# Adapter product between the turns and the scores, the next slot's turn behind the values, q's parts in two pairs of buffers

## The reference

```python
W = weights[condition]; h = einsum('bct,bcd->bdt', x, W)           # style, one 32x32 matrix a batch
qkv = clip(h @ w_qkv.T, -8, 8); q, k = layer_norm(q), layer_norm(k) # over 512 features
scores = q k^T / 4 + alibi bias, causal; probs = softmax(scores)    # 32 heads of 16, 32x32 each
x = x + (probs v) @ w_out.T
y = einsum('bsi,boi->bso', x, weight[adapter_ids])                  # one 512x512 matrix a batch
shared = relu(y @ up_w) ** 2 @ down_w
routed = (y @ fc1 @ expert @ fc2) * sum(top2(y @ gate_w))
x = x + layer_norm(shared + routed)
```

## Time and profile before

| | us |
|---|---|
| median of 3 runs (1119.55 to 1126.66) | 1122.88 |
| the profiled execution | 1121.46 |
| its span, first to last instruction | 1119.7 |
| attention loop, iterations 6 to 30 | 469.47 |

### The profile page before, as it was taken

The page is one execution under the profiler, slowest core; times in us unless marked ns, Lnnn a source line. Parts: engine busy times, 40 slices in busy tenths (PEclk is TensorE's granted clock), DMA queues, the critical chain, the costliest instruction groups (busy, mean ns, idle before and its releaser), DMA issues.

```text
span 1119.7 us, 28302 instructions
## 1 busy us (share of the span) xinstructions
PE 1080.5 (97%) x11396; PEld 874.3 (78%) x11396; DVE 672.4 (60%) x1040; ACT 600.7 (54%) x985; POOL 714.0 (64%) x612
## 2 busy tenths in 40 slices
PE   6999999999999999999998999999999999999994
PEld 4778878788887888877777778787878888787883
DVE  5677667576766677666656245565656565554432
ACT  4567677577776777786866415334161625233220
POOL 4666888788887888888665463555465563533332
PEclk9999999999999999999999999999999999999997
DMA  7125555456555557656467952243315123030101
GB/s 278 41 80 193 196 178 196 167 188 192 186 184 187 187 191 206 193 180 196 151 237 266 346 156 85 85 111 109 97 47 144 49 92 97 29 85 29 47 29 38
DMA packets 95297, 160.84 MB, mean 144 GB/s; under 512 B 46401, under 2 KB 47169, under 8 KB 89793
## 3 DMA queue, kind: packets, MB, share of 16 engines
q1 hardware_dynamic: 79456, 118.16, 32.7%
q0 software_dynamic: 12224, 34.10, 9.6%
q10 hardware_dynamic: 3488, 6.78, 1.7%
HBM read 93.97 MB, written 42.47 MB: 122 GB/s over the span
## 4 chain that ended last, share of the span: by engine, by line
PE 95%; issue 1%; DMA 1%; SPq 1%; DVE 1%; POOL 0%; ACT 0%; DVEq 0%; POOLq 0%
PE banks L675 16%; PE banks L860 16%; PE pair L884 16%; PE bank L675 8%; PE bank L724 7%; PE bank L790 7%; PE banks L877 4%; PE bank L877 4%; PE bank L665 3%; PE banks L790 3%; PE pair L692 3%; PE pair L752 3%; PE banks L830 1%; PE banks L735 1%; PE banks L771 1%
## 5 line engine op out<-in xcount | busy, mean ns | idle before, releaser
L1756 POOL TENSOR_TENSOR w_lo<-w2t,w_hi 128x2048 fp32r<-128x2048 f32 x38 | 174.7, 4598 | 39.4 <-ACT w_hi L1057 36.5
L1826 POOL TENSOR_TENSOR u_lo<-act,u_hi 128x512 fp32r<-128x512 f32 x64 | 82.7, 1292 | 102.6 <-ACT u_hi L1257 102.5
L675 PE MATMUL banks<-wqkv_hi,h_hi 128*128 128x512 f32 x256 | 104.4, 408 | 0.2
L860 PE MATMUL banks<-yT_hi,up_hi 128*128 128x512 f32 x256 | 100.8, 394 | 1.2 <-DMA yT_hi<-y_part_high 1.2
L675 PE MATMUL banks<-wqkv_lo,h_hi 128*128 128x512 f32 x256 | 100.6, 393 | 0.0
L675 PE MATMUL banks<-wqkv_hi,h_lo 128*128 128x512 f32 x256 | 100.5, 392 | 0.0
L860 PE MATMUL banks<-yT_hi,up_lo 128*128 128x512 f32 x256 | 99.8, 390 | 0.0
L860 PE MATMUL banks<-yT_lo,up_hi 128*128 128x512 f32 x256 | 99.6, 389 | 0.0
L884 PE MATMUL pair<-down_hi,u_hi 128*128 128x512 f32 x256 | 99.6, 389 | 0.0
L884 PE MATMUL pair<-down_lo,u_hi 128*128 128x512 f32 x256 | 99.6, 389 | 0.0
L884 PE MATMUL pair<-down_hi,u_lo 128*128 128x512 f32 x256 | 99.6, 389 | 0.0
(11 more groups left out here) (217 smaller groups left out, 3048.3 us busy)
## 6 DMA issues: line engine op xcount, KB each, us to landing
w2t<-in_w SPq DMA_DIRECT2D x38, 1024.0 KB
vx<-v_hl SPq DMA_DIRECT2D x128, 68.0 KB
x1g<-x_rows SPq DMA_DIRECT2D x32, 256.0 KB, 2.9
kx<-k_hl SPq DMA_DIRECT2D x124, 64.0 KB
x_rows<-x1t SPq DMA_DIRECT2D x31, 256.0 KB
ffn_high<-w_high SPq DMA_DIRECT2D x20, 256.0 KB, 3.5
ffn_low<-w_low SPq DMA_DIRECT2D x20, 256.0 KB, 3.6
stage<-in_wqkv SPq DMA_DIRECT2D x3, 1024.0 KB, 9.4
```

The costliest lines, as they stand in the source:

```text
L675: m = e.matmul(into, a[:, c, :], b[:, n, c, :], start=(c == 0 and k == 0), stop=(c == KC - 1 and k == 2))
L860: i = e.matmul((B2, B3)[n % 2], a[:, w, cols], b[m % 2][:, c, :], start=(c == 0 and k == 0), stop=(c == KC - 1 and k == 2))
L1756: e.tensor_tensor(w2_lo[:, :, :], w2t[:, :, :], w2_hi[:, :, :].bitcast(F32), ALU.subtract).then_inc(d_wlo, 1)
L1826: e.tensor_tensor(u_lo[n % FC][:, :], act[n % 2][:, :], u_hi[n % FC][:, :].bitcast(F32), ALU.subtract) \
```

## The change

- On TensorE `adapt_slot(i-6)` moves ahead of `scores(i-2)`; the turn of a slot moves from ahead of `turn_values` to the end of the iteration before, behind `values` (`turn_slot(i-5)` in iteration i, for i from 5 to 29).
- `q_hi`, `q_lo` exist twice; `high_q(t)` and `low_q(t)` wait for `scores(t-2)`.
- `high_chunk` copies to B6 behind `add_x(n)`, and `style` waits for its reader `low_chunk`; the waits on `r_low` at the turns go.
- ScalarE: `slot_in` is the iteration's first; `scale_q` stands ahead of `high_h`; `high_v` behind `high_k`; the planes behind `slot_out`, and their last pair behind `high_o(T-5)`.
- VectorE: `low_slot` stands ahead of `take_k`; `bias_max` behind `low_k`; `low_planes` behind `bias_max`.
- GpSimd: `gather_slot` waits for `style(i+1)` on TensorE and not for `scores(i-2)`; for i = 1 to 3 `style` stands ahead of the gathers.
- SP: `load_planes` behind `load_w2`, `keep_planes` behind `spread_k`.

The diff, with one line of context:

```diff
--- before.py
+++ after.py
@@ -201,8 +201,7 @@
...
     vf = [asb(f"vf{i}", [P, DM]) for i in range(2)]
-    q_hi = asb("q_hi", [P, KC, P], BF16)
-    q_lo = asb("q_lo", [P, KC, P], BF16)
+    q_hi, q_lo = [asb("q_hi0", [P, KC, P], BF16)], [asb("q_lo0", [P, KC, P], BF16)]
 
@@ -304,6 +303,11 @@
...
     u_tiles(range(5, FC))
+    second_q = ExitStack()
+    qsb = tiles_in(second_q)
+    q_hi.append(qsb("q_hi1", [P, KC, P], BF16))
+    q_lo.append(qsb("q_lo1", [P, KC, P], BF16))
+    second_q.close()
     gates = sb("gates", [2 * EXPERTS, TOK])
@@ -575,14 +579,12 @@
...
                     keep_chunk(i - 5)
-                if i >= T - 8:
-                    keep_planes(i - T + 8)
-                if i >= T - 9:
-                    load_planes(i - T + 9)
                 if 0 <= i - 4 < CHUNKS:
...
                     load_w2(i - 5)
+                if i >= T - 9:
+                    load_planes(i - T + 9)
                 if i == 1:
@@ -590,17 +592,19 @@
...
                     spread_k(i - 1)
+                if i >= T - 8:
+                    keep_planes(i - T + 8)
 
...
             load_back(0, 0, 0, 3)
-            keep_planes(EARLY_GROUPS * KC - 1)
             upto(e, "tq", T - 2)
...
             spread_k(T - 2)
+            keep_planes(EARLY_GROUPS * KC - 1)
             upto(e, "tq", T - 1)
@@ -661,6 +665,8 @@
...
                 upto(e, "hlo", t - 1)
+                if t > 5:
+                    e.wait_ge(r_low, min(t - 5, CHUNKS))
                 for c in range(KC):
@@ -697,10 +703,8 @@
...
                 upto(e, "olo", t - 1)
-                if t:
-                    e.wait_ge(r_low, min(t, CHUNKS))
-                if t + 4 > LAG:
-                    e.wait_ge(d_tl, min(t + 4 - LAG, LAST))
+                if t + 4 >= LAG:
+                    e.wait_ge(d_tl, min(t + 5 - LAG, LAST))
                 for b in range(BPT):
@@ -743,8 +747,9 @@
...
                 upto(e, "on", t - 2)
+                hi, lo = q_hi[t % 2], q_lo[t % 2]
                 for c in range(KC):
-                    for k, (a, n) in enumerate(((q_hi, 0), (q_lo, 0), (q_hi, 1))):
+                    for k, (a, n) in enumerate(((hi, 0), (lo, 0), (hi, 1))):
                         for j in range(BPT):
@@ -763,7 +768,6 @@
...
                     upto(e, "olo", s + LAG - 5)
-                    e.wait_ge(r_low, min(s + LAG - 4, CHUNKS))
                 for c in range(KC):
@@ -945,8 +949,6 @@
...
                 project_v(i)
-                if i >= LAG:
-                    turn_slot(i - LAG, banks47)
                 if i >= 4:
@@ -956,16 +958,18 @@
...
                     style(i + 1)
+                if i >= LAG:
+                    adapt_slot(i - LAG, B5)
                 if i >= 2:
                     scores(i - 2)
-                if i >= LAG:
-                    adapt_slot(i - LAG, B5)
                 if i >= 4:
...
                     values(i - 3)
+                if LAG - 1 <= i < T - 2:
+                    turn_slot(i - LAG + 1, banks47)
 
@@ -1045,7 +1049,6 @@
...
                 if slot_halved(s):
-                    upto(e, "ot", s + LAG - 4)
                     e.activation(whole(xgT_hi[:, :]), half(banks47, 0), ACT.Copy).then_inc(d_tc, 1)
@@ -1069,10 +1072,8 @@
...
                 e.activation(w_high[:, :], w_raw[:, :], ACT.Copy).then_inc(r_high, 1)
-                upto(e, "olo", n)
-                if n + 5 > LAG:
-                    e.wait_ge(d_tl, n + 5 - LAG)
-                e.activation(B4, w_raw[:, :], ACT.Copy).then_inc(r_bank, 1)
+                upto(e, "x1", n)
+                e.activation(B6, w_raw[:, :], ACT.Copy).then_inc(r_bank, 1)
 
@@ -1182,8 +1183,8 @@
...
                 upto(e, "qT", t)
-                upto(e, "s", t - 1)
-                e.activation(q_hi[:, :, :].rearrange("p c (g t) -> p c g t", g=ROW_TILES), q_at(t), ACT.Copy) \
+                upto(e, "s", t - 2)
+                e.activation(q_hi[t % 2][:, :, :].rearrange("p c (g t) -> p c g t", g=ROW_TILES), q_at(t), ACT.Copy) \
                     .then_inc(A["qhi"], 1)
@@ -1209,6 +1210,8 @@
...
             for i in range(T - 1):
+                if i >= LAG:
+                    slot_in(i - LAG, banks47)
                 if i < SHORT:
@@ -1222,27 +1225,30 @@
...
                     high_chunk(i - 5)
-                if i >= T - 8:
-                    join_planes(i - T + 8)
-                    high_planes(i - T + 8)
                 if i >= LAG:
...
                     normalize(i - 1)
-                if i >= LAG:
-                    slot_in(i - LAG, banks47)
                 if i >= 4:
                     high_o(i - 4)
-                high_v(i)
-                if i >= SHORT:
+                if i < LAG:
+                    high_v(i)
+                if SHORT <= i < LAG:
                     high_h(i + 1)
...
                     scale_q(i - 1)
+                if i >= LAG:
+                    high_h(i + 1)
+                if i >= 1:
                     scale_k(i - 1)
...
                 if i >= LAG:
+                    high_v(i)
                     slot_out(i - LAG, B5)
+                if i >= T - 8:
+                    join_planes(i - T + 8)
+                    high_planes(i - T + 8)
                 if i >= 2:
@@ -1261,8 +1267,6 @@
...
             high_probs(T - 4)
-            join_planes(EARLY_GROUPS * KC - 1)
-            high_planes(EARLY_GROUPS * KC - 1)
             high_w2(LAST)
@@ -1274,6 +1278,8 @@
...
             high_o(T - 5)
+            join_planes(EARLY_GROUPS * KC - 1)
+            high_planes(EARLY_GROUPS * KC - 1)
             scale_k(T - 2)
@@ -1370,7 +1376,7 @@
...
                 e.wait_ge(r_bank, n + 1)
-                e.tensor_tensor(w_low[:, :], B4, w_high[:, :].bitcast(F32), ALU.subtract).then_inc(r_low, 1)
+                e.tensor_tensor(w_low[:, :], B6, w_high[:, :].bitcast(F32), ALU.subtract).then_inc(r_low, 1)
 
@@ -1378,7 +1384,6 @@
...
                 if slot_halved(s):
-                    upto(e, "ohi", s + LAG - 4)
                     e.tensor_tensor(whole(lo), half(banks47, 0), whole(hi), ALU.subtract).then_inc(d_tl, 1)
@@ -1398,8 +1403,8 @@
...
                     upto(e, "khi", t)
-                upto(e, "s", t - 1)
-                parts = [q[:, :, :].rearrange("p c (g t) -> p c g t", g=ROW_TILES) for q in (q_hi, q_lo)]
+                upto(e, "s", t - 2)
+                parts = [q[t % 2][:, :, :].rearrange("p c (g t) -> p c g t", g=ROW_TILES) for q in (q_hi, q_lo)]
                 e.tensor_tensor(parts[1], q_at(t), parts[0], ALU.subtract).then_inc(A["qlo"], 1)
@@ -1574,25 +1579,27 @@
...
                     low_chunk(i - 5)
-                if i >= T - 8:
-                    low_planes(i - T + 8)
+                if i >= LAG:
+                    low_slot(i - LAG, banks47)
                 take_k(i)
...
                     low_weights(3)
-                if i >= LAG:
-                    low_slot(i - LAG, banks47)
                 if i >= 4:
...
                     low_h(i + 1)
-                if i >= 2:
+                if 2 <= i < LAG:
                     bias_max(i - 2)
...
                     low_k(i - 1, k_hl)
+                if i >= LAG:
+                    bias_max(i - 2)
+                if i >= T - 8:
+                    low_planes(i - T + 8)
                 if i >= 4:
@@ -1792,11 +1799,13 @@
...
                     e.wait_ge(s_tables, 2)
+                if 0 < i < SHORT:
+                    style(i + 2)
                 if i + 3 < T:
...
                     gather_style(i + 3)
-                if i < SHORT:
-                    style(i + 2)
+                if i == 0:
+                    style(2)
                 if i == 0:
@@ -1808,7 +1817,10 @@
...
                 if i >= LAG - 1:
-                    upto(e, "s", i - 2)
+                    if i + 1 < T:
+                        upto(e, "h", i + 1)
+                    else:
+                        upto(e, "s", i - 2)
                     gather_slot(i - LAG + 1)
...
                     subtract_max(i - 2)
```

## The result

The kernel after takes 1173.43 us (median of 4 runs, 1173.03 to 1174.18); the kernel before, beside it, 1122.97 (4 runs, 1119.55 to 1126.66). The ratio is 1.045, with a 95% interval of 1.042 to 1.048. The forecast was 1137, 1118 to 1153: slower was right, and the time lies 36 us over it.

A forecast was written before the change was run, and what follows sets the result against it. It took TensorE, busy 459.46 of 469.47 us in the attention loop, as the bound. Loop +14.5, gather +1.5, slow products −1.6 and tail +0.8 gave +15.2 on 1121.5: 1137, range 1118 to 1153.

The forecast's parts named there:

- A loop through the swapped product, the row maximum and `w_lo`: Attention loop: period 19.6 us through iteration 24, then 18.6, against TensorE's own 18.45; likeliest case, chance 0.74.
- `w_lo` end to product: Loop term: from the end of `w2_lo` on GpSimd to TensorE's first adapter product, 0.21 us.
- bias and row maximum: Loop term on VectorE: from the bias's start to the row maximum's end, 2.53 us.
- row maximum to the next `w_lo` end: Loop term: subtraction, Exp, transpose, copies and `w2_hi` through the end of `w2_lo`, 13.04 us.
- late 11.99: Stretch from row maximum to `w2_lo` end after iteration 24, when no chunk is copied: 11.99 us.
- rival (d): TensorE's clock falls at each recurring 1.1 us wait, slowing the product: +38 us, 1175; chance 0.05.
- scores 1.08: Loop term: scores 0.93 us start to start, plus 0.15 until VectorE starts the bias.
- the gather's start at 3.92 behind `w_lo`'s end: GpSimd's slot gather starts 3.92 us after `w2_lo` ends; used to work out when it lands.
- Product 2.91 and not 2.72: Loop term: the adapter's twelve products on TensorE, forecast at 2.72 us, bounds 2.72 to 2.97.
- Rival (c): Slot's gather lands behind the 1 MB load and decides the period: at 5.5 us landing, 1152; chance 0.09.
- it also fails if VectorE's low_q, low_k hold up the bias: Failure sign on VectorE: these low parts delay the bias, lengthening the loop by their lateness; no size given.
- The stops without a semaphore: Unexplained TensorE waits, about 7 of 10 us; up to 7 could return, most hidden by the loop.

The follow-up runs named there:

- low_last: Kernel after, with the adapter's four products with `w2_lo` last, only those waiting for it, and the `w2t` load waiting for the whole product: 1170.7 us.
- swap_back: Kernel after, with `scores(i-2)` ahead of `adapt_slot(i-6)` again and all else still changed: 1161.6 us.
- before_swap: Kernel before, with only `adapt_slot(i-6)` moved ahead of `scores(i-2)`: 1153.1 us.
- turn_back: Kernel after, with the slot's turn and its readers back at the head of the next iteration's turns, ahead of `turn_values`: 1159.4 us.
- swap_back_bias_first: Kernel after, with scores ahead of the product and bias and row maximum ahead of `low_q`, `low_k` on VectorE; turn still behind `values`: 1144.8 us.
- gather_early: Kernel after, with GpSimd issuing the slot's gather ahead of `reciprocals` and `low_probs`: 1163.4 us.
- gather_after_scores: Kernel after, with the slot's gather waiting for `scores(i-2)` again: 1165.1 us.
- after_gather_early_bias_first: Kernel after, with the gather ahead of `reciprocals` and bias and row maximum first on VectorE; both TensorE moves stay: 1156.6 us.
- before_qk_first: Kernel before, with only VectorE's order changed from iteration 6 on: `low_q` and `low_k` ahead of bias and row maximum: 1162.7 us.

## Why the prediction was right and wrong

**Right.** A loop through the swapped product, the row maximum and `w_lo` sets the period. Its terms, forecast and measured: `w_lo` end to product 0.21, 0.22; bias and row maximum 2.53, 2.55; row maximum to the next `w_lo` end 13.04, 12.96, late 11.99 and 12.31 (the subtraction took 2.28 and not the 1.91 of the earlier trace rows). TensorE waits before its product in nearly every iteration. The clock stays at 1.00, so rival (d) is out in this kernel; that its 1175 lies near is chance. In kernels where TensorE waits longer its mechanism does appear (low_last, swap_back). Alone the loop has 19.7 us (before_swap) where 19.6 was forecast.

**Wrong, the term that carries the miss:** "scores 1.08". The scores with their bias took 2.36, because GpSimd issues the slot's gather inside them. The forecast had the gather's start at 3.92 behind `w_lo`'s end, and the scores from 2.93 to the bias at 4.01 behind it (0.21 + 2.72 + 1.08), and never laid the two beside each other. It costed the gather's new wait by its landing alone. In the kernel before nothing had to keep them apart: the scores stood ahead of the product, and in the earlier trace rows the gather starts with no wait but its own 0.17. With the product ahead, the old wait for the scores would have done it: in before_swap the gather starts 4.7 behind the product's start and the scores have no stop. Product 2.91 and not 2.72 adds 0.19. So the period is 21.0 and not 19.6, and later 20.35 and not 18.6 (there the subtraction's 2.28 adds 0.3 too): 18 × 1.4 + 6 × 1.75 = 36 us, the whole distance from 1137 to 1173. (The sum starts from the profiled execution, 1.4 under the median, and leaves these 1.4 out: by its own terms it is 1138.) The size of the stops is measured, but they couldn't have been worked out from rows: the same issue costs 0.2 plus 0.3 us in turn_back.

**Rival (c) was not a rival, but a second limit.** It was priced with a landing of 4.0 from the earlier trace rows and a bound of 5.1. Where TensorE waits for it, the landing is over the bound: 5.9 in the row of swap_back_bias_first above. In the kernel after, landings of 3.5 to 5.1 us are traced and one of 6.3. They hardly show, because the loop at 21.0 leaves time for them: the turn comes 9.0 behind the product's start and not 7.7. The Trainium skill (DMA: Bandwidth & Descriptors, Anatomy of one DMA) fits about 2.0 us plus bytes over 436 GB/s for a GpSimd DMA, an estimate of 2.6 for the gather's 256 KB; the measured 5.9 includes whatever the load beside it adds.

**Named but not followed:** "it also fails if VectorE's low_q, low_k hold up the bias". In the kernel after they end at 218.92, 1.79 before the bias starts, so the forecast's step held. Without the stops the scores would end some 1.3 earlier, and the margin would be 0.5; in gather_early it is used up in many iterations. With the product behind the scores the bias is held by 4 us. It is the third limit.

**How they combine.** With the other two removed, VectorE's order costs 26 us (1142.1 against 1116.3), the turn 28 (1144.8 against 1116.3) and the swap 35 (1156.6 against 1121.9, where the turn stays behind values but its gather is early). The last two each hold three iterations with the clock at 0.92 or 0.93. Removed from the kernel after one at a time, the swap gives back 12, the turn 14, an earlier gather 10. Loops through the same engines don't add: the longest sets the period, and each of the others waits below it. What comes back on undoing one is made smaller still where the next limit's waits take the clock down.

**The stops without a semaphore** were weighed in the forecast as 7 us to gain. They moved instead: gather_early has 17.1 us of them in values. Counted through the trace, products, weight loads and semaphore instructions together, all of those eleven lie at one place in a block of 256, the 193rd, and ten of them begin 0.2 to 1.4 us behind the start of a transfer on TensorE's instruction queue. The stops in the scores of the kernel before, that of 2.08 us in iteration 11 among them, lie at the same place. So the order of TensorE's work decides which row of small products the place falls into. The work of the other engines decides how long the stop is: the kernel after has TensorE's order of gather_early, and only 0.7 us of stops in values. The Trainium skill (Runtime: NRT & Kernel Launch, Instruction fetch mechanics) calls crossing a block mostly hidden; in a row of 96 small products gather_early's trace has stops of 0.7 to 2.9 us in the open. That the place is where a block ends isn't shown; the spacing of 256 and the transfers fit it.

## What to carry to other kernels

Ask of a wait that is dropped what it would keep apart in time in the new order, and lay the start of every released DMA issue over the other engines' densest stretch. When a move closes a loop, work out the loops that lie just under it as well, since undoing the longest gives back only the distance to the next. An order on VectorE that is free behind late scores costs 26 us in front of early ones: so judge such an order in the place where the stage ahead of it will end. When a period is far over what its waits add up to, read the granted clock of that iteration before looking for another wait.

## What the runs showed of the hardware

- Issuing an indirect DMA on GpSimd (1.16 us) inside 96 small products stopped TensorE by 1.3 us from start to start in most iterations, and by 0.2 in two other kernels with the gather at the same place; with its issue over before the scores there was no such stop. In iteration 27 of the kernel after the gather started behind the scores' last product, and the bias on VectorE still came 0.77 us behind everything that it waited for. Where the gather falls into `out_project` (12 large products in 2.7 us; before_swap, gather_after_scores) no stop is seen.
- A gather of 256 KB with a 1 MB load issued 0.17 behind it was there after 5.9 us; the style gather's median is 4.0.
- Waits of 1.9 to 3.8 us on TensorE were followed by stretches at a granted clock of 0.50 (1.2 GHz) in ten iterations of low_last, where one of 3.1 us wasn't; stops of 1.6 to 2.7 us were in three of after_gather_early_bias_first. Waits of up to 1.7 us in each iteration of the kernel after, and of up to 1.9 in before_swap, left it at 1.00.
- The long stops of TensorE in rows of small products, apart from those at the gather's issue, lie at the same place in a count of its instructions by 256: up to 3.6 us in values (before_qk_first) and 4.9 in the last scores (turn_back). Not every such place has one (0.7 us in all in the kernel after's values, 17.1 in gather_early's, at the same products). TensorE's own order moves them to another row; the other engines' order changes how long they are.
